# Attention with one narrow group of matrix products per two key steps, denominators added up outside PSUM

## The chip, the cores and the metric

The kernel runs on one core of one Trainium2 chip. What counts is the device time of one execution in microseconds (us). The engines are TensorE (PE; PEld is its weight load), VectorE (DVE), ScalarE (ACT), GpSimd (POOL) and SyncE (SP), which here only issues DMAs.

## The reference, cut to what matters

Four sequences of 1024 tokens, 512 wide, go through a conditioned block (layer norms, two small dense nets), then through attention with 16 heads of 32 channels, then through a projection and a last conditioned norm. The change touches attention alone:

```python
energy = jnp.einsum('bhqd,bhkd->bhqk', q, k)
att = jax.nn.softmax(energy, axis=-1) / D ** 0.5
out = jnp.einsum('bhqk,bhkd->bhqd', att, v)
out = jnp.moveaxis(out, 1, 2).reshape(B, N, D)
out = out @ Wp.T + bp
```

## The kernel before

`attention_stage` works through G = 16 groups, each one sequence and four heads. A group has STEPS = 16 steps: for each half of 512 queries, eight blocks of 128 keys. What a step holds on PE:

- **Energies** (`energies`, L1220): four products, one per head, of 128 keys by 512 queries, each into one of two PSUM banks `et[j % 2]`. ACT takes each with `Exp` into `probs` (L1349), a ring of four steps. An energy waits until the exponential of the energy two before it is done.
- **Maxima** (`max_unit`, L1204): the softmax subtracts each query's maximum over all 1024 keys. It comes from separate products, queries by keys, two products of 512 columns to a unit, into one of two double banks `e_ps`. DVE reduces each unit (L1371). Two units (four products) stand in each step, and run LEAD = 13 steps ahead of the energies that use them, so that 26 units come before the first energy. When a half's 16 units are there, `turn_max` (L1213) transposes them on PE into the bank `den_ps`, DVE negates them (L1378, L1380), and SP places the result by DMA as two more rows of the queries (`place_neg`, L1120). This happens at steps 12 and 4 (TURN).
- **Weighted values** (`av`, L1232): four products of 32 output rows, side by side in the four column quarters of PE, with `probs` of the step before, accumulated over eight steps in the bank `av_ps`. ACT copies it out twice a group (`take_av`, L1332).
- **Denominators** (`den`, L1248): POOL adds two steps of `probs` into `psum2` (L1468), and PE multiplies this pair sum with a column of ones, again 32 rows per head. Half of a pair (256 columns, eight instructions) stands in each step, accumulated over a half of the group in the bank `den_ps`. ACT copies it out (`take_den`, L1339), SP spreads it (L1129), DVE inverts it (`invert`, L1387, at steps 5 and 13), SP widens the result (L1140, L1147) and POOL multiplies (L1435 to L1444).

The products with 32 output columns (L1232, L1248, L1213) are called narrow here, the others wide. The order of each engine's work is written out by hand. In a step PE issues: product of a maximum, energy 0, product, energy 1, then the narrow group (`av` of the step before, half of a `den`), then energy 2, product, energy 3, product. The 16 groups run as one first group, a loop of four rounds of three groups, and three last groups; the last has no units of maxima from step 3 on. SP issues at the start of a group the ten loads of the group after next (`load_group`, once `av_done` says that the group before is through), then `store`, `spread_den`, `place_neg`, `widen_rden` in a fixed order; all go to one hardware queue. After attention PE goes on with `project_chunk`.

Of the kernel before, what the change touches and what calls it, by code (L numbers as in the profile page):

```python
# [6 lines left out]
P = 128  # L7
# [3 lines left out]
H, HD = 16, 32  # L11
# [104 lines left out]
def project_chunk(pe, sh, s):  # L116

    a = sh.projection_a[s % A_RING]
    pe.wait_ge(sh.a_loaded[s % A_RING], 16 * KT * (s // A_RING + 1))
    for t in range(TT):  # L120
        acc = sh.ps[4 * (s % 2) + t]
        if s >= 2:

            pe.wait_ge(sh.h1_ready, TT * (s - 2) + t + 1)
        add_bias(pe, sh, acc[:])
# [875 lines left out]
def attention_stage(nc, sh, wp_t):  # L1001
# [11 lines left out]
    with ExitStack() as ctx:  # L1013
# [14 lines left out]
        DEN_STEP = KC // 2 - 1  # L1028
# [32 lines left out]
        den_done, den_taken = sem("at_den_done"), sem("at_den_taken")  # L1061
# [45 lines left out]
        def _(sp):  # L1107
# [46 lines left out]
            def group(g, slot, nth=None, first=False, load=True, with_next=True):  # L1154
# [25 lines left out]
                widen_rden(g, 0)  # L1180

# [14 lines left out]
        def _(pe):  # L1196
# [9 lines left out]

            def turn_max(g, half):

                pe.wait_ge(max_done, UNITS * halves(g, half))
                if not (isinstance(g, int) and g == 0):  # L1210

                    pe.wait_ge(den_taken, halves(g, half) - 2)
                pe.transpose(den_ps[0:UNITS, 0:P], mrow[:, half], sh.ident[:]).then_inc(mrow_turned, 1)  # L1213

            def energies(g, slot, i, j):

                if not (isinstance(g, int) and HG * (STEPS * g + i) + j < 2):

                    pe.wait_ge(exp_done, HG * (STEPS * g + i) + j - 1)
                pe.matmul(et[j % 2][:], ks[0:98, slot, j, (i % KC) * P:(i % KC + 1) * P],  # L1220
                          qs[0:98, slot, i // KC, j, :], start=True, stop=True).then_inc(et_done, 1)
# [14 lines left out]
            def den(g, pair, parts, turned=None):  # L1236
                pe.wait_ge(pair_ready, PAIRS * g + pair + 1)
                n = pair % (KC // 2)
                if n == 0 and not (isinstance(g, int) and g == 0 and pair == 0):

                    pe.wait_ge(den_taken, QH * g + pair // (KC // 2))
                if turned is not None:

                    pe.wait_ge(negt_taken, turned)
                for part in parts:
                    cols = slice(DC * part, DC * (part + 1))
                    for j in range(HG):
                        last = pe.matmul(den_ps[HD * j:HD * (j + 1), cols], ones_col[:], psum2[:, pair % 2, j, cols],  # L1248
                                         start=n == 0 and part == 0, stop=n == KC // 2 - 1 and part == PARTS - 1)
                    if part == PARTS - 1:  # L1250
                        last.then_inc(den_done, 1)

            def den_of_step(g, i, with_next):

                if i == KC // 2:
                    return
                if i == KC // 2 + 1:
                    den(g, 0, range(PARTS), halves(g, 1))
                elif i == KC + KC // 2 + 1:
                    den(g, PAIRS // 2, range(PARTS), halves(g + 1, 0) if with_next else None)  # L1260
                elif i > KC // 2 and i != KC + KC // 2:
                    den(g, (i - KC // 2) // 2, [i % 2])

            def group(g, slot, nth=None, first=False, load=True, with_next=True):
                nxt = (slot + 1) % RING
                prev = (slot + 2) % RING
                for i in range(STEPS):
# [8 lines left out]
                    products = [(unit, keys) for unit in units_of_step(g, slot, i, with_next) for keys in range(2)]  # L1276
                    for j in range(HG):
                        if j < 2:
                            for product in products[j:j + 1]:
                                max_unit(*product)  # L1280
                        energies(g, slot, i, j)
                        if j >= 2:
                            for product in products[j:j + 1]:
                                max_unit(*product)
                        if j == 1:

                            if i >= 1:
                                av(g, slot, i - 1)
                            elif not first:
                                av(g - 1, prev, STEPS - 1)  # L1290
                            if i == TURN[1]:
                                turn_max(g, 1)
                            if with_next and i == TURN[0]:
                                turn_max(g + 1, 0)
                            if i >= KC // 2:
                                den_of_step(g, i, with_next)
                            elif not first:
                                den(g - 1, PAIRS - 2 + i // 2, [i % 2])
# [12 lines left out]
            av(G - 1, RING - 1, STEPS - 1)  # L1311
            den(G - 1, PAIRS - 2, range(PARTS))

            for n in (2, 3):
                for j in range(HG):
                    last = pe.matmul(den_ps[HD * j:HD * (j + 1), :], ones_col[:], probs[:, n, j, :], start=False, stop=n == 3)
            last.then_inc(den_done, 1)
# [4 lines left out]
            project_chunk(pe, sh, 0)  # L1322

        @block.scalar
        def _(act):
# [8 lines left out]
            def take_den(g, half):  # L1334
                act.wait_ge(den_done, KC // 2 * halves(g, half))
                if not (isinstance(g, int) and g == 0):

                    act.wait_ge(den_spread[half], 16 * g)
                nc.scalar.copy(den_sb[:, half], den_ps[:]).then_inc(den_taken, 1)  # L1339

            def group(g, slot, nth=None, first=False, load=True, with_next=True):
                for i in range(STEPS):
# [4 lines left out]
                    for j in range(HG):  # L1347
                        act.wait_ge(et_done, HG * (STEPS * g + i) + j + 1)
                        nc.scalar.activation(probs[:, i % 4, j, :], et[j % 2][:], ACT.Exp).then_inc(exp_done, 1)  # L1349
                        if j == 1 and i == KC:  # L1350
                            take_av(g, 0)
                        if j == 1 and i == 0 and not first:
                            take_av(g - 1, 1)
                    if i == KC // 2 - 1 and not first:
                        take_den(g - 1, 1)
                    if i == KC + KC // 2 - 1:
                        take_den(g, 0)

# [6 lines left out]
            take_den(G - 1, 1)  # L1365

        @block.vector
        def _(dve):
# [4 lines left out]
            def negate_max(g, half):  # L1373
# [4 lines left out]
                nc.vector.tensor_scalar(neg_t[:, HI].bitcast(F32R), den_ps[0:UNITS, 0:P], -1.0, None, ALU.mult).then_inc(negt_hi, 1)  # L1378
                dve.wait_ge(negt_hi, halves(g, half))
                nc.vector.scalar_tensor_tensor(neg_t[:, LO], den_ps[0:UNITS, 0:P], -1.0, neg_t[:, HI], ALU.mult, ALU.subtract).then_inc(negt_taken, 1)  # L1380
# [8 lines left out]
            def group(g, slot, nth=None, first=False, load=True, with_next=True):  # L1389
                for i in range(STEPS):  # L1390
                    units = units_of_step(g, slot, i, with_next)
                    for unit in units[0:1]:
                        take_max(*unit)
# [8 lines left out]
                    if i == KC + DEN_STEP + 2:  # L1402
# [13 lines left out]
            dve.wait_ge(den_taken, halves(G - 1, 1))  # L1416
# [14 lines left out]
        def _(pool):  # L1431
# [14 lines left out]
            def group(g, slot, nth=None, first=False, load=True, with_next=True):  # L1446

                for pair in range(PAIRS if with_next else PAIRS - 1):
                    if not first:
# [12 lines left out]

                    pool.wait_ge(exp_done, HG * (STEPS * g + 2 * pair + 2))
                    if not (first and pair < 2):

                        pool.wait_ge(den_done, PAIRS * g + pair - 1)
                    a = 2 * pair % 4
                    nc.gpsimd.tensor_tensor(psum2[:, pair % 2], probs[:, a], probs[:, a + 1], ALU.add).then_inc(pair_ready, 1)  # L1468

# [280 lines left out]
```

## Time and profile before

| | us |
|---|---|
| median of 3 runs (1995.97 to 1996.78) | 1996.15 |
| the profiled execution | 1994.75 |
| its span | 1992.6 |
| attention in it | about 918 to 1884 |
| one group of 16 steps in its middle | 56.5 |

The page gives for the whole span PE 95% busy, DVE 61%, POOL 58%, ACT 41%. A timeline row gives the start, the length and the engine of a merged run of equal instructions, then line, tiles and count, and in brackets how long the engine sat idle before and what released it. Records of matrix products overlap: the distance between two starts is the time that a product costs, not its length.

### The profile page before, as it was taken

The page shows a single profiled execution, that of the slowest core. Times are in us where ns is not written, and L with a number is a line of the kernel's source. Part 1 is how long each engine was busy: PE and PEld are TensorE (multiplying, and loading weights), DVE is VectorE, ACT ScalarE, POOL GpSimd, SP SyncE. Part 2 cuts the span into 40 slices and gives each one's busy share as a digit, 9 for nine tenths or more (in the row PEclk, how much of TensorE's full clock was granted, in tenths as well). Part 3 has the DMA queues.
Part 4 walks back from the last instruction along what each step waited for, and adds up shares of the span by engine and source line. Part 5 has one row for each costly group of instructions (what it writes and reads, how often), then busy time and mean ns, then how long its engine had stood idle before and what let it go on. Part 6 is the DMA issues. An engine that isn't in the chain of part 4 may idle for free. (4 is left out here: it accounts for less than half of the span.)

```text
span 1992.6 us, 31072 instructions
## 1 busy us (share of the span) xinstructions
PE 1902.4 (95%) x10520; PEld 1243.4 (62%) x10520; DVE 1209.5 (61%) x1510; ACT 809.2 (41%) x1373; POOL 1147.9 (58%) x589
## 2 busy tenths in 40 slices
PE   6599999999998999998999999999999999999995
PEld 1478888888886888885445544554554545554584
DVE  3556555655646554446666666666666666664289
ACT  1322123112312222221566656666666666666300
POOL 0574465466445121212477777777777777877545
PEclk9799999999999999997899999999999999999997
DMA  6301110101123555566344422344443334405293
GB/s 240 123 1 53 45 41 21 53 32 39 35 74 101 190 188 181 189 198 175 73 97 108 103 67 77 96 102 98 107 103 78 78 83 102 107 24 181 92 392 123
DMA packets 117704, 212.67 MB, mean 107 GB/s; under 512 B 18599, under 2 KB 36135, under 8 KB 117577
## 3 DMA queue, kind: packets, MB, share of 16 engines
q1 hardware_dynamic: 98828, 200.04, 33.7%
q10 hardware_dynamic: 18560, 10.94, 1.9%
q8 instruction: 78, 1.28, 0.3%
q14 instruction: 46, 0.37, 0.1%
q0 software_dynamic: 192, 0.05, 0.0%
HBM read 134.40 MB, written 75.80 MB: 105 GB/s over the span
## 5 line engine op out<-in xcount | busy, mean ns | idle before, releaser
L1371 DVE TENSOR_REDUCE at_mrow<-banks 128x1 f32<-128x1024 f32 x512 | 604.4, 1217 | 281.2 <-PE banks L1204 281.2
L1349 ACT ACTIVATE at_probs<-banks 128x512 f32<-128x512 f32 x1024 | 557.6, 597 | 333.7 <-PE banks L1220 314.4
L1468 POOL TENSOR_TENSOR at_pair<-at_probs 128x2048 f32<-128x2048 f32 x127 | 582.0, 4583 | 176.8 <-ACT at_probs L1349 176.7
L1220 PE MATMUL banks<-early_qs,early_ks 98*128 98x512 f32 x1024 | 443.8, 436 | 5.5 <-ACT at_probs L1349 5.5
L1204 PE MATMUL banks<-early_ks,early_qs 96*128 96x512 f32 x1024 | 377.5, 413 | 13.3 <-DVE at_mrow L1371 9.7
L1220 PEld LDWEIGHTS banks<-early_qs,early_ks 98*128 98x128 f32 x1024 | 192.4, 189 | 211.6 <-ACT at_probs L1349 106.8
L1232 PE MATMUL banks<-at_probs,at_v 128*32 128x512 f32 x2048 | 274.9, 609 | 0.9 <-ACT at_probs L1349 0.9
L1204 PEld LDWEIGHTS banks<-early_ks,early_qs 96*128 96x128 f32 x1024 | 199.1, 197 | 53.4 <-DVE at_mrow L1371 26.7
L67 PE MATMUL banks<-l_ht,l_weights 128*128 128x512 f32 x768 | 178.8, 392 | 5.5 <-ACT l_gt L574 5.5
L67 PE MATMUL banks<-qk_nt,l_weights 128*128 128x512 f32 x768 | 177.1, 392 | 3.0 <-ACT qk_gt L889 3.0
L67 PE MATMUL banks<-l_weights,l_hf 128*128 128x512 f32 x768 | 177.3, 390 | 0.0
L574 ACT ACTIVATE l_gt<-banks,mod 128x512 f32<-128x512 f32 x64 | 48.1, 778 | 314.3 <-PE banks L468 278.7
L67 PEld LDWEIGHTS banks<-l_ht,l_weights 128*128 128x128 f32 x768 | 144.6, 189 | 35.6 <-issue 5.8
L67 PEld LDWEIGHTS banks<-qk_nt,l_weights 128*128 128x128 f32 x768 | 145.3, 189 | 33.5 <-ACT qk_gt L889 3.2
L67 PEld LDWEIGHTS banks<-l_weights,l_hf 128*128 128x128 f32 x768 | 143.7, 188 | 29.5
L1248 PEld LDWEIGHTS banks<-at_pair,at_ones_col 128*32 128x32 f32 x2032 | 66.3, 110 | 138.9 <-issue 133.0
L1248 PE MATMUL banks<-at_pair,at_ones_col 128*32 128x256 f32 x2032 | 151.1, 381 | 0.0
L988 POOL TENSOR_TENSOR qk_nt<-qk_gt,qk_nt 128x512 fp32r<-128x512 f32 x32 | 43.0, 1363 | 156.2 <-DVE qk_nt L940 156.2
L898 ACT ACTIVATE qk_out<-banks,cols 128x512 fp32r<-128x512 f32 x64 | 44.1, 690 | 192.5 <-PE banks L67 186.4
L700 POOL TENSOR_TENSOR l_ht<-l_gt,l_ht 128x512 fp32r<-128x512 f32 x64 | 84.3, 1318 | 62.7 <-DVE l_ht L616 62.7
L583 ACT ACTIVATE l_gt<-banks,cols 128x512 f32<-128x512 f32 x96 | 64.7, 689 | 105.0 <-POOL l_hf L700 51.0
L700 POOL TENSOR_TENSOR l_hf<-l_gt,l_hf 128x512 fp32r<-128x512 f32 x64 | 82.7, 1293 | 40.6 <-DVE l_hf L616 40.6
(120 smaller groups left out, 1955.3 us busy)
## 6 DMA issues: line engine op xcount, KB each, us to landing
qk_scratch<-qk_out SPq DMA_DIRECT2D x64, 512.0 KB, 2.8
early_ks<-qk_scratch SPq DMA_DIRECT2D x48, 512.0 KB, 6.7
early_qs<-qk_scratch SPq DMA_DIRECT2D x96, 256.0 KB, 11.6
attn_scratch<-at_out SPq DMA_DIRECT2D x32, 512.0 KB, 2.7
o_a<-attn_scratch SPq DMA_DIRECT2D x32, 512.0 KB, 11.0
v_scratch<-qk_v ACTq DMA_DIRECT2D x32, 256.0 KB, 2.4
at_v<-v_scratch SPq DMA_DIRECT2D x16, 512.0 KB, 14.6
o_x<-x_scratch SPq DMA_DIRECT2D x8, 1024.0 KB, 14.3
```

Of the source, the lines that this page charges most:

```text
L67: last = pe.matmul(out, stationary(a), moving(b), start=start and n == 0, stop=stop and n == len(TERMS) - 1)
L574: nc.scalar.activation(gt[:, k % 2, :], half[k][:], ACT.Identity, bias=sh.mod[:, 2 * which + 1, k, bass.ds(b, 1)], scale=sh.mod[:, 2 * whi ...
L583: nc.scalar.activation(gt[:, n % 2, :], halves[n][:], func, bias=sh.cols[:, col + m:col + m + 1]).then_inc(gt_full, 1)
L700: nc.gpsimd.tensor_tensor(dst[:, LO, i, :], gt[:, i % 2, :], dst[:, HI, i, :].bitcast(F32), ALU.subtract).then_inc(gt_lo, 1)
L898: nc.scalar.activation(qk[:, m, HI, :], ps[m][:], ACT.Identity, bias=sh.cols[:, C_BQ + m:C_BQ + m + 1]).then_inc(qk_hi, 1)
L1204: pe.matmul(e_ps[u % 2][:, keys, :], qs[0:96, slot, half, j, c * P:(c + 1) * P], ks[0:96, slot, j, keys * CH:(keys + 1) * CH], start=True, ...
L1220: pe.matmul(et[j % 2][:], ks[0:98, slot, j, (i % KC) * P:(i % KC + 1) * P], qs[0:98, slot, i // KC, j, :], start=True, stop=True).then_inc ...
L1232: last = pe.matmul(av_ps[rows, :], v[:, slot, kc, rows], probs[:, kc % 4, j, :], start=kc == 0, stop=kc == KC - 1)
L1248: last = pe.matmul(den_ps[HD * j:HD * (j + 1), cols], ones_col[:], psum2[:, pair % 2, j, cols], start=n == 0 and part == 0, stop=n == KC / ...
L1349: nc.scalar.activation(probs[:, i % 4, j, :], et[j % 2][:], ACT.Exp).then_inc(exp_done, 1)
L1371: nc.vector.tensor_reduce(mrow[:, half, u:u + 1], e_ps[u % 2], AX.XY, ALU.max).then_inc(max_done, 1)
L1468: nc.gpsimd.tensor_tensor(psum2[:, pair % 2], probs[:, a], probs[:, a + 1], ALU.add).then_inc(pair_ready, 1)
```

## The change

PE's order is written for two steps at a time. Each pair of steps has one narrow group (`burst`), in its even step, ahead of energy 3: `av` of the two steps before, with a whole `den` between them. Right behind it stand both products of the next unit. The denominator no longer accumulates in PSUM over a half: each pair sum's product goes into a bank that is also an energy bank, and DVE adds it to `den_sb` (`add_den`). The freed bank makes a third energy bank. The transposed maxima use the shared bank too: in the two bursts of a group that turn, the order is transpose, `av`, `av`, `den`, and `den` waits for the negation. LEAD is 12, TURN is steps 12 and 4. ACT's `take_den` is gone. POOL forms the pair sum ahead of its other work. SP's stores stand later in its order.

```diff
-        LEAD = 13
+        LEAD = 12
         SWITCH = STEPS - LEAD
-        TURN = (SWITCH + KC + 1, SWITCH + 1)
+        TURN = (SWITCH + KC, SWITCH)
+        LAG = 2
-        et = sh.ps[0:2]
-        e_ps = [sh.psum[:, 2:4], sh.psum[:, 4:6]]
-        av_ps, den_ps = sh.ps[6], sh.ps[7]
+        et = sh.ps[0:3]
+        e_ps = [sh.psum[:, 3:5], sh.psum[:, 5:7]]
+        av_ps = sh.ps[7]
+        EVEN_SLOTS, ODD_SLOTS, SHARED_SLOT = (0, 1, 2, 1), (2, 0, 1, 2), 0
...
             def spread_den(g, half):
-                sp.wait_ge(den_taken, halves(g, half))
+                sp.wait_ge(den_added, PAIRS // 2 * halves(g, half))
...
                 if not first:
-                    store(g - 1, 0)
                     spread_den(g - 1, 1)
                 place_neg(g, slot, 1)
                 if not first:
                     widen_rden(g - 1, 1)
-                    store(g - 1, 1)
+                    store(g - 1, 0)
                 spread_den(g, 0)
                 if with_next:
                     place_neg(g + 1, (slot + 1) % RING, 0)
                 widen_rden(g, 0)
+                if not first:
+                    store(g - 1, 1)
...
+                e = HG * (STEPS * g + i) + j
+                taken = e - 1 if (i % 2, j) in ((0, 3), (1, 0)) else e - 2
+                if not (isinstance(g, int) and e < 3):
+                    pe.wait_ge(exp_done, taken)
+                if (i % 2, j) == (1, 1) and not (isinstance(g, int) and g == 0 and i // 2 < LAG):
+                    pe.wait_ge(den_added, PAIRS * g + i // 2 - LAG + 1)
...
+            def burst(g, slot, i, first, with_next):
+                if i == 0 and first:
+                    return
+                whose, at, step = (g, slot, i) if i else (g - 1, (slot + 2) % RING, STEPS)
+                pair = i // 2 - LAG
+                turning = i == TURN[1] or i == TURN[0] and with_next
+                turned = None
+                shared_slot_free(g, i)
+                if turning:
+                    turn_max(*((g, 1) if i == TURN[1] else (g + 1, 0)))
+                    turned = halves(g, 1) if i == TURN[1] else halves(g + 1, 0)
+                av(whose, at, step - 2)
+                if turning:
+                    av(whose, at, step - 1)
+                if pair >= 0:
+                    den(g, pair, et[SHARED_SLOT], [psum2[:, pair % 2]], turned)
+                elif not first:
+                    den(g - 1, PAIRS + pair, et[SHARED_SLOT], [psum2[:, pair % 2]])
+                if not turning:
+                    av(whose, at, step - 1)
...
+                    if i % 2 == 0:
+                        products = [(u, keys) for which in range(2) for u in unit(i, which) for keys in range(2)]
+                        for j in range(HG):
+                            for product in products[j:j + 1]:
+                                max_unit(*product)
+                            if j == HG - 1:
+                                burst(g, slot, i, first, with_next)
+                                for u in unit(i + 1, 0):
+                                    for keys in range(2):
+                                        max_unit(u, keys)
+                            energies(g, slot, i, j)
+                    else:
+                        products = [(u, keys) for u in unit(i, 1) for keys in range(2)]
+                        for j in range(HG):
+                            for product in products[j:j + 1]:
+                                max_unit(*product)
+                            energies(g, slot, i, j)
...
-            def take_den(g, half):
...
+            def add_den(g, pair, bank=et[SHARED_SLOT]):
+                half, n = divmod(pair, PAIRS // 2)
+                dve.wait_ge(den_done, PAIRS * g + pair + 1)
+                if n == 0:
+                    if not (isinstance(g, int) and g == 0):
+                        dve.wait_ge(den_spread[half], 16 * g)
+                    nc.vector.tensor_copy(den_sb[:, half], bank[:]).then_inc(den_added, 1)
+                else:
+                    dve.wait_ge(den_added, PAIRS * g + pair)
+                    nc.vector.tensor_tensor(den_sb[:, half], bank[:], den_sb[:, half], ALU.add).then_inc(den_added, 1)
...
-                    for unit in units[0:1]:
+                    for unit in units[0:2]:
                         take_max(*unit)
                     if i == TURN[1]:
                         negate_max(g, 1)
                     if with_next and i == TURN[0]:
                         negate_max(g + 1, 0)
-                    for unit in units[1:2]:
-                        take_max(*unit)
-                    if i == DEN_STEP + 2 and not first:
+                    pair = i // 2 - LAG
+                    if i % 2 == 0 and pair >= 0:
+                        add_den(g, pair)
+                    elif i % 2 == 0 and not first:
+                        add_den(g - 1, PAIRS + pair)
+                    if i == 5 and not first:
                         invert(g - 1, 1)
```

At the end, both last `av` and one `den` over the pair sum and the two last tiles of `probs` stand ahead of `project_chunk`.

## Rows read from the trace of the kernel before

**Rows 1.** Busy us by stretch: PE, PEld, DVE, ACT, POOL; then PEclk, DMA.
```profile
1200.00:1300.00 100.00, 100.00 (x687) 50.28 (x686) 68.21 (x68) 64.99 (x121) 77.25 (x25) 1.00 0.30 78
1835.00:1845.00 10.00, 8.55 (x56) 3.06 (x59) 0.25 (x1) 7.11 (x13) 5.68 (x3) 1.00 0.17 49
```

**Rows 2.** Groups of instructions, 1200 to 1600 us: busy, mean ns of one, idle before.
```profile
L1371 DVE TENSOR_REDUCE at_mrow<-banks 128x1 f32<-128x1024 f32 x223 | 263.3, 1217 | 129.4 <-PE banks L1204 129.4
...
L1349 ACT ACTIVATE at_probs<-banks 128x512 f32<-128x512 f32 x446 | 242.7, 597 | 137.8 <-PE banks L1220 127.2
```

**Rows 3.** Waits, 1200 to 1600 us: total, times, longest.
```profile
PEld banks L1220 <- ACT at_probs L1349: 41.0, 218, 0.2
```

**Rows 4.** Timeline, one step of the middle on PE: start, length, line.
```profile
1319.67 0.50 PE L1220 MATMUL banks<-early_qs,early_ks 98*128 98x512 f32 x1
1320.01 0.40 PE L1204 MATMUL banks<-early_ks,early_qs 96*128 96x512 f32 x1
1320.24 0.40 PE L1220 MATMUL banks<-early_qs,early_ks 98*128 98x512 f32 x1
...
1321.43 0.42 PE L1220 MATMUL banks<-early_qs,early_ks 98*128 98x512 f32 x1
1321.78 1.07 PE L1232 MATMUL banks<-at_probs,at_v 128*32 128x512 f32 x8
1322.66 0.61 PE L1248 MATMUL banks<-at_pair,at_ones_col 128*32 128x256 f32 x8
1323.21 0.50 PE L1220 MATMUL banks<-early_qs,early_ks 98*128 98x512 f32 x1
```

**Rows 5.** Timeline, the same step on ACT and DVE.
```profile
1320.21 2.27 ACT L1349 ACTIVATE at_probs<-banks 128x512 f32<-128x512 f32 x4 [1.25 <-PE banks L1220]
...
1320.91 2.36 DVE L1371 TENSOR_REDUCE at_mrow<-banks 128x1 f32<-128x1024 f32 x2 [1.05 <-PE banks L1204]
```

**Rows 6.** Timeline, a step of the last group, without maxima.
```profile
1841.88 0.30 PEld L1220 LDWEIGHTS banks<-early_qs,early_ks 98*128 98x128 f32 x2 [0.41 <-issue]
...
1842.41 1.08 ACT L1349 ACTIVATE at_probs<-banks 128x512 f32<-128x512 f32 x2 [0.23 <-PE banks L1220]
...
1843.55 0.19 PEld L1220 LDWEIGHTS banks<-early_qs,early_ks 98*128 98x128 f32 x1 [0.30 <-ACT at_probs L1349]
...
1843.98 1.06 PE L1232 MATMUL banks<-at_probs,at_v 128*32 128x512 f32 x8
```

**Rows 7.** Timeline, a step of the first group, which has no denominators yet.
```profile
964.79 1.07 PE L1232 MATMUL banks<-at_probs,at_v 128*32 128x512 f32 x8
965.78 0.50 PE L1220 MATMUL banks<-early_qs,early_ks 98*128 98x512 f32 x1
```

**Rows 8.** Timeline, the end of attention on PE.
```profile
1865.18 1.06 PE L1232 MATMUL banks<-at_probs,at_v 128*32 128x512 f32 x8
...
1869.17 1.05 PE L1248 MATMUL banks<-at_pair,at_ones_col 128*32 128x256 f32 x16
1870.03 1.90 PE L1316 MATMUL banks<-at_probs,at_ones_col 128*32 128x512 f32 x16
1871.86 0.50 PE L61 MATMUL banks<-bias_rows,ones 128*128 128x512 f32 x1
```

**Rows 9.** Timeline, the negation of a half's maxima on DVE.
```profile
1312.58 0.28 DVE L1378 TENSOR_SCALAR at_neg_t<-banks 16x128 fp32r<-16x128 f32 x1
1312.89 0.28 DVE L1380 SCALAR_TENSOR_TENSOR at_neg_t<-banks,at_neg_t 16x128 f32<-16x128 f32 x1
```

**Rows 10.** Timeline, PE before the first energy.
```profile
938.45 2.35 PE L1204 MATMUL banks<-early_ks,early_qs 96*128 96x512 f32 x4 [0.19 <-DVE at_mrow L1371]
```

**Rows 11.** DVE groups, last stage: an addition of a bank and an SBUF tile.
```profile
L1568 DVE TENSOR_TENSOR o_h<-banks,o_x 128x512 f32<-128x512 f32 x32 | 21.8, 681 | 6.5 <-PEq L1013 6.5
```

**Rows 12.** Timeline, one group: first load issued, inversion of the spread denominators.
```profile
1241.83 1.34 SPq L91 DMA_DIRECT2D early_ks<-qk_scratch  x3
...
1262.01 0.24 DVE L1387 RECIPROCAL at_rden_c<-at_den_c 128x16 f32<-128x16 f32 x1
```

More of the change, by code:

```diff
@@ L124, in project_chunk @@
             pe.wait_ge(sh.h1_ready, TT * (s - 2) + t + 1)
+        if bank_free is not None and t == 2:
+            pe.wait_ge(*bank_free)
         add_bias(pe, sh, acc[:])
@@ L1234, in av, with den @@
                 last.then_inc(av_done, 1)
-            def den(g, pair, parts, turned=None):
+            def den(g, pair, bank, sums, turned=None):
                 pe.wait_ge(pair_ready, PAIRS * g + pair + 1)
-                n = pair % (KC // 2)
-                if n == 0 and not (isinstance(g, int) and g == 0 and pair == 0):
-                    pe.wait_ge(den_taken, QH * g + pair // (KC // 2))
                 if turned is not None:
                     pe.wait_ge(negt_taken, turned)
-                for part in parts:
+                for part in reversed(range(PARTS)):
@@ L1246, in den @@
                     cols = slice(DC * part, DC * (part + 1))
[L1247 to L1255, printed above, removed]
-                    return
[L1257 to L1262, printed above, removed]
+                    for n, tile in enumerate(sums):
+                        for j in range(HG):
+                            last = pe.matmul(bank[HD * j:HD * (j + 1), cols], ones_col[:], tile[:, j, cols],
+                                             start=part == PARTS - 1 and n == 0, stop=part == 0 and n == len(sums) - 1)
@@ L1272, in group, with unit @@
                         pe.wait_ge(stack_loaded[nxt], LOADS * (nth + 1))
-                    products = [(unit, keys) for unit in units_of_step(g, slot, i, with_next) for keys in range(2)]
-                    for j in range(HG):
-                        if j < 2:
+                    def unit(step, which):
+                        return units_of_step(g, slot, step, with_next)[which:which + 1]
+                    if i % 2 == 0:
+                        products = [(u, keys) for which in range(2) for u in unit(i, which) for keys in range(2)]
+                        for j in range(HG):
                             for product in products[j:j + 1]:
                                 max_unit(*product)
-                        energies(g, slot, i, j)
-                        if j >= 2:
+                            if j == HG - 1:
[6 more added lines that the diff above has]
+                        products = [(u, keys) for u in unit(i, 1) for keys in range(2)]
+                        for j in range(HG):
                             for product in products[j:j + 1]:
                                 max_unit(*product)
[L1285 to L1298, printed above, removed]
+                            energies(g, slot, i, j)
             pe.wait_ge(stack_loaded[RING - 1], 16 * STACK_LOADS)
@@ L1310, in _ @@
             groups(pe, group)
[L1311 to L1317, printed above, removed]
+            for i in (STEPS - 2, STEPS - 1):
+                av(G - 1, RING - 1, i)
+            den(G - 1, PAIRS - 2, et[2], [psum2[:, 0], probs[:, 2], probs[:, 3]])
             pe.wait_ge(wp_lo, 1)
@@ L1364, in _ @@
             take_av(G - 1, 1)
-            take_den(G - 1, 1)
         @block.vector
@@ L1415, in _ @@
             groups(dve, group)
-            dve.wait_ge(den_taken, halves(G - 1, 1))
+            add_den(G - 1, PAIRS - 2, et[2])
+            dve.wait_ge(den_added, PAIRS * G - 1)
             dve.wait_ge(out_hi, halves(G - 1, 1) - 2)
@@ L1448, in group @@
                 for pair in range(PAIRS if with_next else PAIRS - 1):
+                    pool.wait_ge(exp_done, HG * (STEPS * g + 2 * pair + 2))
+                    if not (first and pair < 2):
+                        pool.wait_ge(den_done, PAIRS * g + pair - 1)
+                    a = 2 * pair % 4
+                    nc.gpsimd.tensor_tensor(psum2[:, pair % 2], probs[:, a], probs[:, a + 1], ALU.add).then_inc(pair_ready, 1)
                     if not first:
@@ L1461, in group @@
                         multiply(g, 0)
[L1463 to L1468, printed above, removed]
             nc.gpsimd.memset(ks[96:98, 0:RING - 1].bitcast(F32), 1.0).then_inc(ones_ready, 1)
```

39 lines of the change are left out of this document (14 added, 25 removed).

## The prediction

> **What bounds the kernel now.** I read the busy times by stretch first. In the middle of attention PE is busy in all of 100 us at full clock, with ACT at 65 and DVE at 68; in the last group, which has no maxima, PE idles 1.4 us in 10 and still runs at full clock [rows 1]. That says "PE", and a change that takes overhead off PE should pay. But a busy engine need not be the only limit, so I went on to the waits: 218 of the 446 energies there have their weight load released by an exponential, never more than 0.2 us late [rows 3]. ACT is close behind PE although it idles a third of the time.
>
> The timeline shows why. A step on PE is 3.53 us from energy 2 to the next energy 2. Wide products come every 0.23 us; energy 1 to `av` is 0.35, `av` to `den` 0.88, the half `den` to energy 2 0.55, and the wide product after that 0.34 [rows 4]. So each narrow group costs about 0.12 on the way in and 0.12 + 0.11 on the way out, beyond its own work.
>
> The second loop goes through ACT. In the last group an energy's weight load comes at 1841.88 and its exponential starts at 1842.41, 0.53 later; two exponentials span 1.08 us and one lasts 0.597 [rows 2, 6], so the second starts 0.49 after the first. The second ends at 1843.50, the load it frees comes 0.05 later (1843.55), and `av` 0.43 after that [rows 6]. Then 0.88 for `av` and 0.55 for `den`: 0.53 + 0.49 + 0.60 + 0.05 + 0.43 + 0.88 + 0.55 = 3.53. The step takes 3.53 us without the four maxima products too. **Both loops, PE's own and the one through two energy banks and ACT, have the same length today.** What the change does to each has to be worked out apart.
>
> **A plain pair of steps after the change, PE alone.** Sixteen wide products, two `av`, one whole `den`. From the energy behind the burst (call it E3) to the last wide product ahead of the next burst are 13 x 0.234 = 3.04; in, 0.33; `av` 0.88; both halves of a `den` and the handover to the next narrow product 0.86 (1869.17 to 1870.03) [rows 8]; `av` with the way out, 0.99 [rows 7]; then 0.34 and 0.23 to E3. Sum 6.67, against 2 x 3.53 = 7.07. The handover from `den` to `av` inside a group has no row; the nearest is that one, between narrow products, which costs nothing above 2 x 0.43. At most it is a way out, 0.12. I take 0.01.
>
> **The same pair through ACT.** During a burst ACT has only what lies in the three energy banks. The eighth energy from E3 (E10) needs the bank of E7, and E3 to E7 are five exponentials in a row. E3 to its exponential is 0.45 (1321.43, and the last of four that end at 1322.48 after 0.60 [rows 4, 5]); four more starts at 0.49 are 1.97; end and load 0.65; then 0.43 + 0.23 to `av`, since a maxima product lies between. From `av` on, as above: 0.88 + 0.86 + 0.99 + 0.34 + 0.23. Sum 7.03, with roundings 7.03 to 7.05; with the 0.01, 7.05. So **PE loses 0.4 us of work per pair and the exponentials give back nearly all of it**: a third bank buys 0.49 per pair in the loop, and doubling the burst costs that. Per pair -0.02; about 120 pairs have maxima: -2.4 us, between -5 and, if the handover costs 0.12, +11.
>
> The Trainium skill (TensorEngine Tiling (Array Packing), Tiling Modes) says that changing the tiling mode drains TensorE. The ways in and out agree. By that rule alone the time would be that of rival B.
>
> **Turning bursts.** Now `den` waits for the negation inside its burst; before, a step without `den` lay between. Take E10's load as zero. `av` is due at 0.66, and after two of them `den` at 2.42, or 2.45 with 0.03 for the transpose of 128 columns, half a half `den` at most (bounds 0 and 0.2, and all of it inside DVE's time below). The even step's first unit is complete with the product behind E8, two exponentials earlier: -0.99 + 0.08 + 0.23, and 0.43 to DVE (the product behind 1320.24 + 0.23 is reduced from 1320.91 [rows 4, 5]), so -0.25. Its reduction takes 1.14, the second's 1.14 (two span 2.36, one 1.22 [rows 2, 5]), then 0.31 + 0.28 for the negation [rows 9], 0.05 and 0.09 for semaphore and load: 2.76. The stall is 0.3, in all 0.34 for each of 31 turns: +10.5 us. Queued behind it on PE are E3 and all after it, so nothing hides it: ACT is idle by then.
>
> **Both ends.** Two units less ahead of the first energy: each is 1.27 us, as four products and the idle are 2.54 [rows 10]; -2.5, of which 0.2 goes again in the first group. In the last group, from step 4 on, a pair without maxima is 0.53 + 1.97 + 0.65 + 0.43 + 0.88 + 0.86 + 0.99 = 6.3. Before, from the step-0 `av` to the projection: 15 x 3.53 + 6.68 = 59.7 [rows 8]. After: two pairs of 7.05, the turn's 0.3, five of 6.3, then from the last burst 2.73 + 0.53 + 1.97 + 0.65 to the last `av`, 0.88, and three tiles of denominators, 3 x 0.86 + 0.11: 55.4; its step-0 burst stands 0.7 later in the step. -3.6 us.
>
> **Edits I cost at nothing, with their cover.** `add_den`: 0.68 us for a bank and an SBUF tile, beside POOL's work [rows 11]. It starts about 1.3 us ahead of E3 and ends 0.7 ahead; DVE's next unit is ready 0.2 behind E3. DVE then has 4 x 1.14 + 0.7 = 5.3 in 7.05 us; if a unit came 0.3 us late, PE would wait for its bank. `take_den` off ACT: ACT idles there. POOL: 4.6 for a pair sum and 1.3 for one other operation in 7 us, covered; its products and SP's stores come later, with a half group to spare. The loads now start some 1.8 us later after the burst's start, as `av_done` stands at its end.
>
> **Sum**: -2.4 + 10.5 - 2.3 - 3.6 = +2.2. On the profiled execution, 1994.75, that is 1997; its median stands 1.4 higher, so **1998**. What the measurement can tell from no change is about 0.2%, 4 us.
>
> **The rivals.**
> *A, the forecast:* both loops at 7.05, the turns paid. For it: the ACT loop adds up to 3.53 today from single rows, at a step with and without maxima. Chance 0.66, its own range 1989 to 2007.
> *B, PE's pace decides:* if the third bank lets ACT keep up during bursts, a pair is 6.67 and the gain 0.38 x 120 = 46 us more, 1952. Against it: five exponentials at 0.49 between E3 and E10 are hard arithmetic. Half of it (a shorter exponential chain by 0.2) gives 1974. Chance 0.14 for both.
> *C, slower: the inversion on DVE.* `invert` at step 5 waits for a small DMA behind the next loads on one queue. Today it comes 20.2 us after the first load's issue [rows 12], just as DVE turns to it. Now the loads start about 1.8 us later, and add_den and the maxima of PE's next burst stand behind the inversion. The store of 0.5 MB, which today lies between 3.5 MB of loads and that DMA, goes behind it, which gives 20.2 x 0.5 / 4 = 2.5 back. By this it lands in time. It decides once it comes over 2 us later than that: each further us costs each of 13 groups 1 us; with 1 us, 2011, with 2, 2024. Chance 0.20.
>
> **How the numbers follow.** Within A the sum stands between the bounds -9 and +11: same in half, slower in a third, faster in the rest (0.33, 0.21, 0.12 of the whole). B is faster, 0.14 less a little that ends as no change; C slower, 0.17, and 0.03 no change. Faster 0.24, same 0.38, slower 0.38. The range 1980 to 2013 leaves out B's full gain and C's far end.
>
> **What would show it.** Right: the timeline shows pairs of 7.05 us from burst to burst, energies E6 to E10 at 0.49 with their weight loads released by ACT, PE busy below 96% in the middle, and turning pairs 0.3 longer with `den` (now behind two `av`) released by DVE. Wrong: pairs of 6.7 with PE at 100% (B); a stall of PE once per group behind step 5, with DVE's inversion waiting for `at_den_c` (C); the way into or out of `den` within the burst over 0.1.

## The result, and the profile after

The changed kernel takes **2004.23 us** (median of 6 runs, 2003.35 to 2006.67), the kernel before 1995.39 beside it: ratio 1.0043, 95% interval 1.0032 to 1.0054. It is slower by 8.8 us, some 6 more than the forecast of 1998 and inside its range. The profiled execution took 2005.06 us, its span is 2003.1.

Busy times by stretch, from the windows of the changed kernel (PE, PEld, DVE, ACT, POOL, then granted clock, DMA):

```profile
1200.00:1300.00 100.00, 99.65 (x679) 50.84 (x678) 77.71 (x83) 58.56 (x117) 76.51 (x24) 1.00 0.36 89
1835.00:1845.00 10.00, 9.71 (x52) 4.13 (x50) 3.61 (x5) 7.01 (x15) 8.00 (x5) 1.00 1.03 401
```

The middle looks as it did before [rows 1], except that ten points of DVE came and six of ACT went. The share of PE says nothing of its spare time here: the records of its products stretch over small gaps. The waits, 1200 to 1600 us, say more:

```profile
PEld banks L1229 <- ACT at_probs L1351: 53.1, 248, 0.3
...
DVE at_rden_c L1395 <- DMA at_den_c<-at_den_sb: 10.5, 7, 1.8
```

More energies' loads wait for an exponential than before [rows 3]. One plain pair of steps, from its timeline, with the next burst's start:

```profile
1265.29 1.07 PE L1241 MATMUL banks<-at_probs,at_v 128*32 128x512 f32 x8
...
1266.17 1.05 PE L1255 MATMUL banks<-at_pair,at_ones_col 128*32 128x256 f32 x16
...
1267.03 1.04 PE L1241 MATMUL banks<-at_probs,at_v 128*32 128x512 f32 x8
...
1268.00 0.73 PE L1208 MATMUL banks<-early_ks,early_qs 96*128 96x512 f32 x2
...
1268.58 0.39 PE L1229 MATMUL banks<-early_qs,early_ks 98*128 98x512 f32 x1
...
1269.01 4.03 ACT L1351 ACTIVATE at_probs<-banks 128x512 f32<-128x512 f32 x8 [2.97 <-PE banks L1229]
...
1272.29 1.07 PE L1241 MATMUL banks<-at_probs,at_v 128*32 128x512 f32 x8
```

`av` to `den` is 0.88, `den` 0.86, second `av` to the wide product 0.97, the next energy (E3) 0.58 behind that: 3.29, where the prediction has 3.31. The first exponential follows E3 after 0.43, and eight run without a gap from 1269.01 to 1273.04. **The pair is 7.00 us** from burst to burst.

A turning burst of the same group:

```profile
1257.80 0.27 PE L1218 MATMUL banks<-ident_sb,at_mrow 128*16 128x128 f32 x1
...
1258.00 1.92 PE L1241 MATMUL banks<-at_probs,at_v 128*32 128x512 f32 x16
...
1259.28 0.27 DVE L1374 TENSOR_SCALAR at_neg_t<-banks 16x128 fp32r<-16x128 f32 x1
1259.59 0.28 DVE L1376 SCALAR_TENSOR_TENSOR at_neg_t<-banks,at_neg_t 16x128 f32<-16x128 f32 x1
...
1260.01 1.07 PE L1255 MATMUL banks<-at_pair,at_ones_col 128*32 128x256 f32 x16
```

`den` stands 2.01 behind the first `av`; two `av` alone are 1.76. The stall is about 0.25 to 0.3, and the pairs after turning bursts are 7.29.

**Where the 8.8 us come from.** A *crossing* is a place where the loop jumps back to its start; a *straight* group is one that stands in code without a loop. I took the start of each group's first energy from the trace, all 16 groups in both kernels (us from one to the next; the last number runs to the first product of the projection):

```
before: 57.43 56.54 56.54 59.05 58.10 56.54 58.88 58.04 56.54 59.01 56.51 56.54 56.54 56.53 56.53 | 60.54
after:  57.04 56.70 56.77 61.07 59.26 56.76 60.42 59.80 56.77 60.84 58.10 56.76 56.84 57.24 57.27 | 59.33
```

From the first maxima product to the first energy the time fell from 33.37 to 30.83, -2.5. An ordinary group in the loop went from 56.54 to 56.76, +2.7 over the twelve of the loop; groups 13 and 14, straight code behind the loop, +1.4; group 0 -0.4; the last group -1.2. That makes 0. The rest stands in the long groups, 3 and 4, 6 and 7, 9 and 10: there the loop over rounds of three groups jumps back. Beyond six ordinary groups these cost **10.4 us before and 18.9 after: +8.5, the whole loss of this stage** (8.6; the two profiled spans lie 10.5 apart, because the one after also reaches attention 2.0 later). The timeline after, at the third jump:

```profile
1531.67 1.13 PE L1229 MATMUL banks<-early_qs,early_ks 98*128 98x512 f32 x3
...
1536.49 0.65 PE L1208 MATMUL banks<-early_ks,early_qs 96*128 96x512 f32 x1 [3.69 <-issue]
...
1537.60 0.60 ACT L1351 ACTIVATE at_probs<-banks 128x512 f32<-128x512 f32 x1 [3.87 <-PE banks L1229]
```

And before:

```profile
1525.74 0.39 PE L1204 MATMUL banks<-early_ks,early_qs 96*128 96x512 f32 x1
...
1526.17 1.22 DVE L1371 TENSOR_REDUCE at_mrow<-banks 128x1 f32<-128x1024 f32 x1 [1.17 <-PE banks L1204]
...
1528.36 0.49 PE L1204 MATMUL banks<-early_ks,early_qs 96*128 96x512 f32 x1 [2.22 <-DVE at_mrow L1371]
```

```profile
1181.00:1190.00 9.00, 8.74 (x49) 4.18 (x49) 3.58 (x3) 4.38 (x9) 4.78 (x2) 0.81 0.48 112
1354.50:1363.50 9.00, 8.73 (x49) 4.55 (x49) 3.58 (x3) 4.54 (x9) 4.82 (x2) 0.81 0.57 119
1528.00:1537.00 9.00, 8.64 (x56) 4.40 (x60) 4.88 (x5) 5.77 (x11) 5.70 (x3) 1.00 0.59 133
```
```profile
1182.00:1191.00 9.00, 8.50 (x44) 4.40 (x45) 3.55 (x4) 2.57 (x5) 3.53 (x2) 0.64 0.02 5
1359.00:1368.00 9.00, 8.96 (x44) 4.53 (x45) 3.59 (x4) 2.60 (x5) 3.64 (x2) 0.62 0.02 5
1536.00:1545.00 9.00, 8.51 (x48) 4.71 (x49) 4.83 (x5) 3.85 (x8) 3.62 (x2) 0.81 0.07 25
```

The two prices are about equal, and together nearly the whole +8.5. PE stood for 6.6 us at the three jumps before and for 10.7 after, +4.1. The groups that follow a jump (4, 7 and 10) are 3.0 us over ordinary ones before and 6.9 after, +3.9; where the clock stayed at 1.00, in group 10 of the kernel before, there is no excess at all (56.51).

The Trainium skill (Runtime: NRT & Kernel Launch, Instruction fetch mechanics) says that a taken branch to a target outside the fetched window stalls until its page is there. The long record of the three taken jumps and the short one of the jump not taken agree; that the time is the fetch is that page's claim; no run here separates it from another cause.

### The profile page after: what moved, and what is told of

It is laid out like the page before. It is cut to its first block and busy times, and to the rows that moved or that the text cites. A ratio compares the mean times of both kernels' runs of the same rounds, so it can differ in the third digit from the quotient of the medians.

```text
span 2003.1 us, 31532 instructions
## 1 busy us (share of the span) xinstructions
PE 1908.8 (95%) x10536; PEld 1256.4 (63%) x10536; DVE 1296.0 (65%) x1637; ACT 758.5 (38%) x1341; POOL 1146.8 (57%) x589
## 5 line engine op out<-in xcount | busy, mean ns | idle before, releaser
L1351 ACT ACTIVATE at_probs<-banks 128x512 f32<-128x512 f32 x1024 | 518.6, 625 | 336.4 <-PE banks L1229 336.1
L1208 PE MATMUL banks<-early_ks,early_qs 96*128 96x512 f32 x1024 | 411.8, 427 | 17.3 <-issue 10.7
L1229 PE MATMUL banks<-early_qs,early_ks 98*128 98x512 f32 x1024 | 412.1, 426 | 3.7 <-ACT at_probs L1351 1.3
L1208 PEld LDWEIGHTS banks<-early_ks,early_qs 96*128 96x128 f32 x1024 | 189.8, 197 | 136.7 <-issue 95.2
L1241 PE MATMUL banks<-at_probs,at_v 128*32 128x512 f32 x2048 | 266.7, 604 | 0.0
L1255 PE MATMUL banks<-at_pair,at_ones_col 128*32 128x256 f32 x2032 | 135.9, 385 | 2.7
L618 DVE CAST l_ht<-l_gt 128x512 fp32r<-128x512 f32 x64 | 52.0, 813 | 89.9 <-ACT l_gt L585 48.5
L1388 DVE TENSOR_TENSOR at_den_sb<-banks,at_den_sb 128x512 f32<-128x512 f32 x95 | 65.5, 690 | 68.0 <-PE banks L1255 68.0
```

The source lines that it names most:

```text
L618: nc.vector.tensor_copy(dst[:, HI, i, :], gt[:, i % 2, :]).then_inc(gt_hi, 1)
L1208: pe.matmul(e_ps[u % 2][:, keys, :], qs[0:96, slot, half, j, c * P:(c + 1) * P], ks[0:96, slot, j, keys * CH:(keys + 1) * CH], start=True, ...
L1229: pe.matmul(et[(EVEN_SLOTS, ODD_SLOTS)[i % 2][j]][:], ks[0:98, slot, j, (i % KC) * P:(i % KC + 1) * P], qs[0:98, slot, i // KC, j, :], sta ...
L1241: last = pe.matmul(av_ps[rows, :], v[:, slot, kc, rows], probs[:, kc % 4, j, :], start=kc == 0, stop=kc == KC - 1)
L1255: last = pe.matmul(bank[HD * j:HD * (j + 1), cols], ones_col[:], tile[:, j, cols], start=part == PARTS - 1 and n == 0, stop=part == 0 and ...
L1351: nc.scalar.activation(probs[:, i % 4, j, :], et[(EVEN_SLOTS, ODD_SLOTS)[i % 2][j]][:], ACT.Exp).then_inc(exp_done, 1)
```

## The experiments

Theory **J**: the jump back, no longer hidden behind queued products, costs the 8.5. Theory **T**: the turns do. From e5 on, T stands for another rival (every third group is long for reasons of its own, jump or not), and F for one more; both are given in the expectations.

**e1, PE's jump behind the burst of step 0** (PE alone; the other engines' code stays):

```
-            groups(pe, group)
+            group(0, 2, nth=0, first=True)
+            group(1, 0, part="head")
+            with pe.Fori(0, 4) as k:
+                for i in range(RING):
+                    group(3 * k + i + 1, i, nth=k + (i + 2) // RING, part="tail")
+                    group(3 * k + i + 2, (i + 1) % RING, part="head")
...
```

> PE's loop over the groups is turned so that its jump back stands right behind the burst of a group's step 0 (and the unit of maxima behind it) and no longer behind energy 7 of step 15; nothing else changes. Theory J (the jump): PE's jump takes 3.7 us in both kernels, the kernel before hides 1.5 us of it under work already queued, the changed one nothing, since its sequencer has just waited for an exponential; the three jumps cost 18.9 us in the changed kernel and 10.4 before. With a burst of 2.7 us queued in front of it, most is hidden: 13 to 17 us less than the changed kernel, some 1987 to 1991, ratio to before 0.996 to 0.998. Rival T (turning bursts and the pairs themselves make the loss; a jump costs what it costs wherever it stands): within 3 us of the changed kernel, ratio 1.003 to 1.005.

Measured 1999.04 us, 1.0017 (1.0008 to 1.0026), 5 us less than the changed kernel: more than T allows, far less than J said. The timeline shows why:

```profile
1530.35 1.58 ACT L1364 ACTIVATE at_probs<-banks 128x512 f32<-128x512 f32 x3 [2.21 <-issue]
...
1530.99 1.07 PE L1241 MATMUL banks<-at_probs,at_v 128*32 128x512 f32 x8 [2.08 <-ACT at_probs L1364]
...
1536.06 0.50 PE L1229 MATMUL banks<-early_qs,early_ks 98*128 98x512 f32 x1 [1.61 <-issue]
```

At its new place PE's jump costs 1.6 of idle time here and 0.2 and 0.5 at the other two, not 3.2 to 3.8. But ACT has a stop of its own behind its jump, 2.2 to 2.4 us, which would before have fallen into the time that PE stood; now PE waits for it. The waits, 1150 to 1700 us:

```profile
PE banks L1241 <- ACT at_probs L1364: 6.6, 3, 2.3
PE banks L1229 <- issue: 2.4, 3, 1.6
...
ACT at_probs L1364 <- issue: 6.9, 3, 2.4
```

PE's idle time fell only from 10.7 to 9.0, and the crossings still cost 14.4 us in all. So the queue ahead of the jump hides it, as J says, but J left out that the other engines stop too.

**e2, the negation between the two reductions of its step** (DVE):

```
-                    for unit in units[0:2]:
+                    for unit in units[0:1]:
                         take_max(*unit)
...
                         negate_max(g + 1, 0)
+                    for unit in units[1:2]:
+                        take_max(*unit)
```

> DVE takes the negation of the maxima between the two units of the turning step again, as the kernel before did; all else is the changed kernel. Theory D (den waits in its burst for the second unit's reduction, which stands ahead of the negation on DVE): the 0.30 us in each of 31 turns go, 9 us less than the changed kernel, some 1995, ratio to before 0.999 to 1.001. Rival W: the unit behind the negation now comes later, and the wait moves to the maxima products behind the burst: no gain, ratio 1.003 to 1.005.

Measured 1993.63, 0.9987 (0.9978 to 0.9996). The negation is done before the second `av` begins:

```profile
1253.06 1.92 PE L1241 MATMUL banks<-at_probs,at_v 128*32 128x512 f32 x16
...
1253.58 0.28 DVE L1376 SCALAR_TENSOR_TENSOR at_neg_t<-banks,at_neg_t 16x128 f32<-16x128 f32 x1
...
1254.80 1.05 PE L1255 MATMUL banks<-at_pair,at_ones_col 128*32 128x256 f32 x16
```

`den` is now 1.74 behind `av` and not 2.01; a group is 56.16 with pairs of 7.11 (the one that ends with a transpose) and 7.00 or 6.99. The stall of 0.30 is gone whole. Note what this means for the attribution: without the turning stall, and with all its jumps, the changed kernel is no slower than the kernel before. Measured from the kernel before, the stall and the jumps are each as large as the whole loss; only against the prediction, which had the stall in its sum, are the jumps the missing part.

**e3, both edits.**

> Both edits of the two runs above. If J and D hold and are independent, the gains add up: 22 to 26 us less than the changed kernel, 1978 to 1982, ratio to before 0.991 to 0.994. If T and W hold: as the changed kernel.

Measured 1990.8, 0.9972 (0.9962 to 0.9983): the two effects nearly add (-13.4 against -5.2 and -10.6), but the sum is far short of the 22 to 26 expected, because e1's part was.

**e4, exponentials of 448 columns in place of 512.** The last 64 queries of each tile of probabilities are left out and stay 1, set once.

```
-nc.scalar.activation(probs[:, i % 4, j, :], et[...][:], ACT.Exp)
+nc.scalar.activation(probs[:, i % 4, j, 0:448], et[...][:, 0:448], ACT.Exp)
```

> The changed kernel, but every exponential takes 448 of its 512 columns (the other 64 hold ones, so the output is another). PE's work is unchanged. Theory A (the loop through three energy banks and five exponentials in a row sets the pair, PE alone would need 6.67 us): an exponential starts 0.05 to 0.06 us sooner after the last, so the pair falls from 6.99 by 0.25 to 0.3, down to PE's floor at most: 28 to 38 us less than the changed kernel, ratio to before 0.985 to 0.991. Rival B (PE's own pace sets the pair): within 3 us of the changed kernel.

Measured 1989.21, 0.9967 (0.9954 to 0.998): -15 us, about half of what was expected, the plain pair 6.86. So ACT is in the loop, but only four starts of the chain from E3 to E7 count, and they went from 1.92 to 1.81, no more, because the first three energies come 0.47 apart from PE itself, one maxima product between each. Eight together:

```profile
1269.33 3.67 ACT L1351 ACTIVATE at_probs<-banks 128x448 f32<-128x448 f32 x8 [0.18 <-PE banks L1229]
```

3.67 against 4.03 above. The wide products here still take 3.24 from E3 to the last, not the 3.04 of PE alone; by the prediction's sum of 6.67 for PE alone, which no run measured, the rest of 0.19 is what ACT still holds.

**e5 and e6, the loop over rounds written out,** in the changed kernel and in the kernel before; nothing else differs.

```
-            with eng.Fori(0, 4) as k:
+            for k in range(4):
```

> The changed kernel with its loop over rounds written out: all sixteen groups stand one behind the other as straight code, no engine jumps within attention. Theory J (the loss is what the three jumps back cost): the three crossings, 18.9 us beyond an ordinary group in the changed kernel, go; twelve groups take the 57.25 us that its straight groups 13 and 14 showed in place of 56.76, +6; so about -13, near 1991. Rival T (the lengthened groups come from the order of the work in every third group, the ring's reloading above all): those groups stay long, the time stays at 2004 or rises by the 6. Rival F (straight code has to be fetched too): the 18.9 goes but is given back in stops spread over the groups, 2000 to 2010.

> The kernel before with its loop over rounds written out in the same way. Theory J: its three crossings cost 10.4 us beyond an ordinary group, and its straight groups 13 and 14 take 56.5 like the ones in the loop; so -10, near 1986, and the changed kernel written out would be slower than it by some 5 us (0.3 per cent: turns and straight groups), not by the 9 of the two loops. Rival T: stays at 1996. Rival F: somewhere between 1990 and 2000, with stops spread over the groups.

Measured **1991.71** (0.9977, 0.9967 to 0.9987) and **1984.3** (0.9939, 0.9925 to 0.9953). The long groups are gone in both: every group of e5 is 57.27 but for the first, the last and two of 57.5 (they recur in e8 and not in e9, and were not followed up), every one of e6 between 56.53 and 56.55 but for the first and the last. The granted clock, too, is 1.00 from 1150 to 1700 us in both. PE's own waits, 1150 to 1700 us, in the changed kernel (first fence), in the kernel before, and in e5 (e6 has none):

```profile
PE banks L1208 <- issue: 10.7, 3, 3.8
```
```profile
PE banks L1204 <- DVE at_mrow L1371: 6.6, 3, 2.3
```
```profile
PE banks L1229 <- ACT at_probs L1351: 0.3, 1, 0.3
```

J is shown: T and F would have left the groups long or spread the stops. The changed kernel lost 18.9 less the 6 that straight groups cost, 12.5 measured; the kernel before lost 12.2, 10.4 by the groups; the kernel before's profiled execution lay 1.7 under the median of its runs beside e6. Without any jump the change still costs 7.4 us: a straight group is 0.73 longer than one of e6, two turns at 0.44 each, less 0.02 for each of eight pairs. Its plain pairs are 7.05 where the loop's code has 6.99, which e9 takes up.

**e7, six groups to a round,** one jump back in place of three.

```
-            with eng.Fori(0, 4) as k:
-                for i in range(RING):
-                    group(3 * k + i + 1, i, nth=k + (i + 2) // RING)
+            with eng.Fori(0, 2) as k:
+                for i in range(2 * RING):
+                    group(6 * k + i + 1, i % RING, nth=2 * k + i // RING + (i % RING + 2) // RING)
```

> The changed kernel with six groups to a round and two rounds: one jump back in place of three, the groups still loop code. Theory J: two of three crossings go, 12 to 13 us, groups stay at 56.76: near 1991.5, and one long group left (about 60.5 to 61). Rival T (every third group is long for its own reasons): four long groups stay, 2004. Rival F (a longer body costs fetches inside it): less than 6 us gained.

Measured 1993.18 (0.9983, 0.9974 to 0.9993). One place is left with 61.43 and 59.23, 7.1 beyond two ordinary groups (the branch record here is 4.26 us); all others in the loop are 56.7 to 56.9. The cost goes with the number of jumps.

**e8, written out, the early negation, and the inversion one step later:**

```
-                    if i == 5 and not first:
+                    if i == 6 and not first:
                         invert(g - 1, 1)
```

> The changed kernel written out, with the negation between the two reductions of its step on VectorE, and with the inversion of the previous group's second half one step later (step 6, behind that step's denominators), so that its wait on the denominators' transfer has no addition queued behind it. If the parts add: -13 for the jumps, -9.5 for the negation (groups of 56.65 in place of 57.25), and -1 to -1.5 in the last group, where the VectorE wait for the spread denominators had held one pair up by 0.35: about 1980, ratio to the kernel before near 0.992. If the jumps and the negation fill the same gap: no lower than 1985. If the late inversion delays the chain of the outputs instead: the last group grows by 1 or more.

Measured 1983.01, 0.9935 (0.9921 to 0.9949). Groups are 56.62 to 56.64 and the last one 58.66 in place of 59.61, so both parts did what was said; the sum came out 3 short of 1980, as the profiled execution's first group is 0.6 longer, and the rest was not followed up.

**e9, as e8, with the waits of a step's first exponential turned:**

```
-                        act.wait_ge(av_done, STEPS * g + i - 3)
-                        act.wait_ge(pair_ready, PAIRS * g + (i - 4) // 2 + 1)
+                        act.wait_ge(et_done, HG * (STEPS * g + i) + 1)
+                        act.wait_ge(pair_ready, PAIRS * g + (i - 4) // 2 + 1)
+                        act.wait_ge(av_done, STEPS * g + i - 3)
                     for j in range(HG):
-                        act.wait_ge(et_done, HG * (STEPS * g + i) + j + 1)
+                        if j > 0 or first and i < 4:
+                            act.wait_ge(et_done, HG * (STEPS * g + i) + j + 1)
```

> The written-out kernel with the early negation and the late inversion, and one more edit: the first exponential of a step states its three waits in the other order (energy first, the two for its buffer behind it). In the trace of the written-out kernels such an exponential is preceded by a separate semaphore instruction that holds the energy's wait, and starts 0.55 us after the one ahead of it, where the loop's code needs 0.49. Theory W (this order is what makes straight groups 57.27 against 56.77 in the loop): the pair goes from 7.05 to 6.99, a group from 56.63 to about 56.15, 14 groups, so -6 to -7: near 1976, ratio to the kernel before 0.990. Rival (the order of the waits isn't what decides which of them the instruction itself carries, or the longer distance has another cause): groups stay at 56.63, the time at 1983.

Measured **1972.39 us, 0.9879 (0.9861 to 0.9896)**, 24 us under the kernel before and the fastest of all. The groups are 56.11. ACT's timeline of a pair in e5 and in e9:

```profile
1264.23 4.08 ACT L1351 ACTIVATE at_probs<-banks 128x512 f32<-128x512 f32 x8 [2.99 <-PE banks L1229]
```
```profile
1265.37 4.03 ACT L1353 ACTIVATE at_probs<-banks 128x512 f32<-128x512 f32 x8 [0.27 <-PE banks L1229]
```

Of three waits the exponential carries one itself and a semaphore instruction ahead of it the others. In e5 the carried one was `av_done`, long met, and the separate one held the energy: the exponential starts 0.546 after the one before (0.546 to 0.557 over 75 pairs). In e9 the exponential carries the energy and the separate one passes early: 0.494. The 0.05 lies between E3 and E7 and is paid at each pair. That is 14 x 0.5 = 7 us by the groups, and between the profiled executions of e8 and e9 it is 6.7 (1983.08 to 1976.41). The other runs of e9 lie 4 lower than its profiled one; their mean granted clock was 0.976 to 0.977, its own 0.972, so more than these 7 us must not be put down to the waits. Why the three waits fall out so, and differently in the loop's code, no run shows.

With the jumps, the turning stall and this wait out of the way, the new order is 12 us faster than the old one written out (0.9879 against 0.9939 of the kernel before). The old order had no such repairs beyond the written-out loop; its exponentials in e6 already start 0.494 apart.

## Why the prediction came out as it did

**Both loops of 7.05: right.** The plain pair is 6.99 or 7.00 in the loop and 7.05 in straight code. From `av` to E3 the sum is off by 0.02; four starts of exponentials are 1.92 and not 1.97, since behind the second they come every 0.476 and not 0.49. e4 shows ACT's part. The prediction expected PE's busy share to fall below 96%, and it did not; the pace of the pairs decides it. Per pair that is -0.075, not -0.02: over the 120 pairs about -9 (-8 with the 7.05 of the straight groups), where the term was -2.4. The bounds of this term, -5 and +11, were later used as if they were nearly those of the whole sum (-9 and +11); with the other three terms its upper end would have been about +16, or 2012, still inside the stated range.

**The turning stall: right in mechanism and size, the transpose was mis-sized.** 0.30 stall as predicted, shown by e2. But the transpose was put at 0.03, and pairs with one are 0.11 to 0.12 longer than plain ones: a tile of another shape, 128x16, stands ahead of `av`, and the way from the maxima product to `av` grows from 0.33 to 0.44. That the shape is what costs was not tested. 30 turns cost 0.41 each, 12.3, where 31 were put at 10.5; the one in the last group, with no further units for DVE to reduce, is without the stall (pairs of 7.09 and 6.35).

**The start: right,** -2.5 and group 0 another -0.4 (predicted -2.3 in all).

**The last group: -1.2, not -3.6.** Rival C's wait does occur here, though not in the middle. DVE in the last group of the changed kernel:

```profile
1848.72 0.25 DVE L1395 RECIPROCAL at_rden_c<-at_den_c 128x16 f32<-128x16 f32 x1 [6.35 <-DMA at_den_c<-at_den_sb]
1848.89 0.63 DVE L1388 TENSOR_TENSOR at_den_sb<-banks,at_den_sb 128x512 f32<-128x512 f32 x1
...
1849.67 0.93 PE L1229 MATMUL banks<-early_qs,early_ks 98*128 98x512 f32 x3 [1.03 <-DVE at_den_sb L1388]
```

The addition behind the inversion comes late, the energy that needs the shared bank waits for it (PE stands for 1.03), and that pair is 7.11, not 6.35. e8 took the wait away: all its pairs without maxima are 6.35 to 6.5, and its last group is 0.95 shorter than e5's. Near the end the granted clock fell as well, with PE busy all the while:

```profile
1872.00:1876.00 4.00, 4.00 (x33) 1.36 (x26) 0.69 (x1) 0.37 (x1) 4.00 (x2) 0.68 0.37 147
```

It fell for a few us in the last group of every run with the changed order, and in neither of the two with the old one; why stays open. In the middle the inversion waits up to 1.8 us too, but this is absorbed: the pair with it is as long as the others.

**The missing term.** The step that failed is the sum itself, "-2.4 + 10.5 - 2.3 - 3.6": it has no entry for the three places where the loop jumps back. The prediction went through queues on DVE, POOL and SP, but not through what PE's own sequencer has queued where its stream breaks. The rows were there: three idle times of 2.2 us on PE, 6.6 in all, in the trace of before. The change put those jumps behind energies that wait, and that is +8.5: 4.1 of it idle time, about as much the lower clock behind it. All that the sum did name comes to 0 by the groups, where it said +2.2; the misses in it (pairs 6.6 better, turns 1.8 and last group 2.4 worse, straight groups) nearly cancel. The 8.8 of the medians is the missing term. So the forecast came within 6 us with one term left out, and that it came so near is partly luck: its other errors cancelled. That was rival A with one more price; no rival named it.

## What to carry to other kernels

Before a loop's order of work is changed, look at its jump back: find the engine with the long branch, and how much work it has queued ahead of it. Behind a burst of work whose weight loads do not wait the jump cost less (e1), but each engine has a jump of its own, and moving one uncovers the next; where the program's size allows, write the loop out. And where an instruction has several waits, look in the trace at which one it carries; here it paid to let it carry the one that comes last.

## What the hardware showed that I had not expected

- A taken jump on PE takes 3.3 to 4.8 us by its record (4.76 in e4), 3.2 to 4.7 of idle PE where nothing is queued; the same jump not taken, 83 ns. On ACT the record is 53 ns, but in e1 its next exponential came 2.2 to 2.4 us late with nothing else to wait for.
- After 3.2 to 3.8 us of idle PE at a jump, the 9 us behind it had a mean granted clock of 0.62, 0.64 and 0.81; after 2.1 and 2.3 us it was 0.81, and after another stop of 2.2 us 1.00. The length of the stop alone does not say whether the clock falls.
- Exponentials of 128x512 that follow without a gap start every 0.476 us (the first two starts 0.494 apart) while their records grow from 0.597 to 0.67. Record lengths are no cadence.
- The order in which three waits are written in the program is worth 0.05 us on each pair, 7 us of this kernel by its groups.
